# The halves of P exchanged between VectorE and GpSimd, and GpSimd's small work spread

## The chip, the core and the metric

One core of a Trainium2 chip runs the whole program. The metric is the device time of one execution in microseconds; the medians are over several runs. TensorE (PE in the profile) multiplies, VectorE (DVE), ScalarE (ACT) and GpSimd (POOL) work on elements, and SyncE (SP) issues nearly all DMAs. Each engine takes its instructions in the order in which the program has them, and waits for the others by semaphores that count up.

## What is computed

A cross attention with 16 heads over 64 batches of 128 queries (dimension 128) and 120 context rows, and behind it a feed-forward layer with 8 experts, in which each expert takes the 32 best tokens of a batch:

```python
q = _split_heads(queries @ Wq.T, N_HEAD, D_KEY)
k = _split_heads(keys @ Wk.T, N_HEAD, D_KEY)
v = _split_heads(values @ Wv.T, N_HEAD, D_VALUE)
scores = jnp.einsum('bhqd,bhkd->bhqk', q, k) * D_MODEL ** (-0.5) + attn_bias
weights = jax.nn.softmax(scores, axis=-1)
out = jnp.einsum('bhqk,bhkd->bhqd', weights, v)
...
gating, idx = jax.lax.top_k(affinity, k)
x_in = x[bidx, idx]
h = jax.nn.silu(jnp.einsum('bekd,eid->beki', x_in, w_gate)) * jnp.einsum('bekd,eid->beki', x_in, w_up)
...
x = x + _L0_xattn_ref(_layernorm(x, axis=-1), ctx_1024, ctx_1024, fside_1x1xSxS2_0, ...)
x = x + _L0_ffn_ref(_layernorm(x, axis=-1), ...)
```

## The kernel before

**Halves.** To multiply in float16 at nearly the precision of float32, a value is split into an upper half, its cast to float16, and a lower half, the value less the upper one. A product is then three matmuls. The names end in `_hi` and `_lo`. P (the exponentials of the scores, `probs`) and O (the attention's output, `o_sb`) are split as well, and both halves of both lie in one tensor `parts` for each of four groups, which a DMA transposes into `w_f` (`turned`).

**Batches, groups, steps.** The attention stage runs over slots t, one for each batch; in a slot four steps g = 0 to 3, one for each group of four heads. The scores and P of batch t - 1 are made in slot t. `behind(t, g, k)` is the group that lies k steps behind: O = PV runs 4 steps behind P (`PV_LAG`), its split 5, the projection 8. Slots up to 4 are written out, those from 5 to 62 are a loop that does two in a pass, and the last are written out again. Each engine has its own `step` or `slot`, and its order is the order of that code:

- **SyncE** (`turn`, L228; `load_x`, L207; `load_ffn`, L218). In slot t: turn(t, 0), load x and ctx of batch t + 2, turn(t, 1), load a piece of the experts' weights, turn(t, 2), turn(t, 3). `turn` of group g waits for the lower half of P of that group (`p_lo_ready`) and of the O that goes with it, and for what is still read from the place that it writes.
- **VectorE** (L454). Step 0 begins with bn_stats of x of batch t + 1 (L464), which waits for `loaded_xc`, both loads of that batch. Every step has four fused operations that make `neg` (scale, bias and row minimum, L472, with a read of the accumulator each); step 0 then has the aggregates mv (L488), step 1 xn (L494) and, for an earlier batch, xn2 (L536), and every step the reciprocal of P's row sums, v_lo (L514), o_sb (L522) and, last, the lower half of P of the group one step behind (L542).
- **GpSimd** (L298). In slot t, one after the other: the lower half of O (`lower_o`), eps added to the variance (vpe), rstd by a power, ctx_hi, the scaled piece of weights wsc (L326), the upper half of P of group 0 (`upper_parts`, L287), O again, ctx_lo, xn_hi, xn_lo, P of group 1, O, ffn_hi, xg_hi, P of group 2, O, ffn_lo, xg_lo, P of group 3. It waits for its own results by the counter `pool_chain`, whose values `chain` works out.
- **ScalarE** (L391). In each step v_hi and qk from PSUM, the upper half of O (L419), and four Exp for P (L443), which wait for `neg` and for the lower half of the group two steps back, in whose buffer they write. Steps 3 and 0 have copies for the transposes and the logits.
- **TensorE** (L579). In each step the scores (L590), V, the projection, PV and then Q and K.

Behind the attention stage (to about 743 us) come the routing and the experts' stage (from about 786 us to the end). There the subtract of 128x512 elements (L1133) runs on GpSimd.

Of the kernel before, what the change touches and what calls it, by code (L numbers as in the profile page):

```python
# [5 lines left out]
ALU = mybir.AluOpType  # L6
# [67 lines left out]
def attention(nc, v):  # L74
# [8 lines left out]
    with ExitStack() as ctx:  # L83
# [177 lines left out]
        @block.gpsimd  # L261
        def _(pool):
            pool.memset(ident[:, :], 0.0).then_inc(pool_chain, 1)
            pool.memset(half[:, :], -0.5).then_inc(const_ready, 1)
            pool.memset(vpe[:, :], 1.0).then_inc(const_ready, 1)
            pool.memset(mv[:, :, :], 1.0).then_inc(const_ready, 1)
            for i in range(2):
                pool.memset(v_hi[i][:, :, DH:OW], 1.0).then_inc(const_ready, 1)
            for i in range(GROUPS):
                pool.memset(parts[i][:, :, :], 0.0).then_inc(const_ready, 1)  # L270
            pool.wait_ge(pool_chain, 1)
            pool.affine_select(out=ident[:, :], in_=ident[:, :], compare_op=ALU.not_equal, fill=1.0,
                               base=0, pattern=[[-1, 128]], channel_multiplier=1).then_inc(const_ready, 1)
            pool.iota(iota[:, :], pattern=[[1, 128]], base=0, channel_multiplier=0,
                      allow_small_or_imprecise_dtypes=True).then_inc(const_ready, 1)
            pool.wait_ge(const_ready, 11)
            pool.tensor_copy(ident_h[:, :], ident[:, :]).then_inc(ident_h_ready, 1)

            def upper_parts(t, g):

                if live(t - 1):
                    n = 4 * (t - 1) + g
                    pool.wait_ge(probs_ready, n + 1)
                    if some(t - 1):
                        pool.wait_ge(moved[g], 16 * (t - 1))
                    alone(pool)
                    pool.tensor_copy(p_parts[g][:, 0, :, 0:K], probs[g % 2][:, :, :]).then_inc(p_hi_ready, 1)  # L287

            def lower_o(t, g):

                b5, g5 = behind(t, g, SPLIT_LAG)
                if live(b5):
                    n = 4 * b5 + g5
                    pool.wait_ge(o_hi_ready, n + 1)
                    pool.tensor_tensor(o_parts[g5][:, 1, :, :], o_sb[g5 % 2][:, :, :], o_parts[g5][:, 0, :, :],  # L295
                                       ALU.subtract).then_inc(o_lo_ready, 1)

            def slot(t, par):  # L298
                c = chain(t)
                at = slice(t * WCH, (t + 1) * WCH) if isinstance(t, int) else bass.ds(t * WCH, WCH)  # L300
                i = (par + 1) % 2
                lower_o(t, 0)

                pool.wait_ge(stats_ready, t + 2)
                alone(pool)
                pool.tensor_scalar(vpe[:, :], mv[:, :, 1], EPS, None, ALU.add).then_inc(pool_chain, 1)
                pool.wait_ge(pool_chain, c[0])
                if some(upto(t + 1)):
                    pool.wait_ge(xn_ready, upto(t + 1))
                if some(t - 4):  # L310
                    pool.wait_ge(xn2_ready, t - 4)
                pool.tensor_tensor(rstd[:, :], vpe[:, :], half[:, :], ALU.pow).then_inc(rstd_ready, 1)
                if live(t + 1):

                    pool.wait_ge(loaded_xc, (t + 2) * 32)
                    if some(4 * t):
                        pool.wait_ge(v_written, 4 * t)
                    alone(pool)
                    pool.tensor_copy(ctx_hi[i][:, :], ctx_f[i][:, :]).then_inc(pool_chain, 1)
                if live(t):  # L320

                    if some(t):
                        pool.wait_ge(ffnw_ready, t)
                    pool.wait_ge(loaded_ffn, (t + 1) * 16)
                    alone(pool)
                    pool.tensor_scalar(wsc[:, :], wst[par][:, :], WSCALE, None, ALU.mult).then_inc(pool_chain, 1)  # L326
                upper_parts(t, 0)
                lower_o(t, 1)
                if live(t + 1):

                    pool.wait_ge(pool_chain, c[1])
# [8 lines left out]
                    pool.wait_ge(pool_chain, c[3])  # L340
# [3 lines left out]
                if live(t):  # L344

                    pool.wait_ge(pool_chain, c[2])
                    alone(pool)
                    pool.tensor_copy(ffn_hi[:, at], wsc[:, :]).then_inc(pool_chain, 1)
                if live(t - 4):

                    pool.wait_ge(xn2_ready, t - 3)
                    alone(pool)
                    pool.tensor_copy(xg_hi[:, t - 4, :], xn2[:, :]).then_inc(pool_chain, 1)
                upper_parts(t, 2)
                lower_o(t, 3)
                if live(t):
                    pool.wait_ge(pool_chain, c[4])
                    pool.tensor_tensor(ffn_lo[:, at], wsc[:, :], ffn_hi[:, at], ALU.subtract).then_inc(ffnw_ready, 1)
                if live(t - 4):
                    pool.wait_ge(pool_chain, c[5])  # L360
                    pool.tensor_tensor(xg_lo[:, t - 4, :], xn2[:, :], xg_hi[:, t - 4, :],
                                       ALU.subtract).then_inc(xg_ready, 1)
                upper_parts(t, 3)

            def chain(t):

                def before(lag, each):
                    return each * (t - lag) if not isinstance(t, int) else each * min(max(t - lag, 0), B)  # L370
                c = 1 + (t + 1) + before(-1, 2) + before(0, 2) + before(4, 1)
                out = [c + 1]
                for batch in (t + 1, t, t + 1, t, t - 4):
                    out.append(out[-1] + (1 if live(batch) else 0))
                return out

            slots(pool, slot)

        @block.scalar
        def _(act):  # L380
# [10 lines left out]
            def step(t, par, g):  # L391
# [42 lines left out]
                if gw == GROUPS - 1 and live(tw - 4):  # L434
                    act.wait_ge(logits_written, tw - 3)
                    nc.scalar.copy(logits[:, tw - 4, :], gate_out).then_inc(logits_ready, 1)
                if live(t - 1):

                    act.wait_ge(neg_ready, n + 1)
# [11 lines left out]
        def _(dve):  # L451
            dve.wait_ge(const_ready, 11)

            def step(t, par, g):  # L454
# [10 lines left out]
                if live(t - 1):  # L465
# [5 lines left out]
                    for i in range(GH):  # L471
# [38 lines left out]
                if live(tw):  # L510
# [3 lines left out]
                    nc.vector.tensor_tensor(v_lo[pw][0:K, at, :],  # L514
                                            bk_b[gw % 2][0:K, 0:GH * DH].rearrange("p (a b) -> p a b", a=GH),
                                            v_hi[pw][0:K, at, 0:DH], ALU.subtract).then_inc(v_lo_ready, 1)
                if live(b4):

                    dve.wait_ge(rsum_ready, 4 * b4 + g4 + 1)
# [10 lines left out]
                if g == 1 and live(t - 4):  # L530
# [7 lines left out]
                b1, g1 = behind(t, g, 1)  # L538
                if live(b1):
# [746 lines left out]
```

## Time and profile before

| | us |
|---|---|
| Median of three runs | 1086.35 (1084.44 to 1086.76) |
| The profiled execution | 1088.91, of it the span 1086.8 |
| TensorE busy | 1003.1 (92% of the span) |
| VectorE busy | 900.8 (83%) |
| GpSimd busy | 881.3 (81%) |
| ScalarE busy | 811.6 (75%) |

Instructions overlap at their ends: the next one on an engine starts 0.04 to 0.1 us before the recorded end of the one ahead. What one costs in a row of instructions is therefore read from start to start. A wait is given with what ended it. S0 below is the start of bn_stats in step 0 of a slot.

### The profile page before, as it was taken

How to read it: one execution, taken by the hardware profiler on the slowest of the kernel's cores; microseconds unless marked ns; L12 is line 12 of the kernel's file. 1: busy time of each engine (PE TensorE's matmuls, PEld its weight loads, DVE VectorE, ACT ScalarE, POOL GpSimd, SP SyncE). 2: the span in 40 equal slices, each digit the busy share in tenths (PEclk: the TensorE clock that was granted, in tenths of full speed). 3: DMA queues.
4: the chain of work that ended last, by engine and by line, in shares of the span. 5: the costliest groups of instructions: out<-in, count | busy, mean ns of one | idle time of the engine just before them, and what ended most of it. 6: DMA issues, size and time to landing. Idle time of an engine off the chain costs nothing. (4 is left out here: it accounts for less than half of the span.)

```text
span 1086.8 us, 47397 instructions
## 1 busy us (share of the span) xinstructions
PE 1003.1 (92%) x13640; PEld 810.8 (75%) x13640; DVE 900.8 (83%) x3848; ACT 811.6 (75%) x2408; POOL 881.3 (81%) x1411
## 2 busy tenths in 40 slices
PE   4889999999999999999999999984799999999995
PEld 3777888888888888888888888873366666666664
DVE  4999999999999999999999999994756565665553
ACT  5887888888888888888888888871476667566562
POOL 7789999999999999999999999983077767677673
PEclk9999999999999999999999999995599999999998
DMA  3998887888888887888888888882001121111112
GB/s 101 161 152 157 162 167 154 169 160 163 162 159 163 165 164 154 166 160 162 161 160 162 164 167 158 170 153 49 1 21 29 30 67 30 39 55 32 50 49 68
DMA packets 440585, 130.91 MB, mean 120 GB/s; under 512 B 417504, under 2 KB 433888, under 8 KB 440544
## 3 DMA queue, kind: packets, MB, share of 16 engines
q1 hardware_dynamic: 439680, 128.24, 60.7%
q10 hardware_dynamic: 864, 2.16, 0.6%
q8 instruction: 21, 0.34, 0.1%
q14 instruction: 20, 0.16, 0.1%
HBM read 16.58 MB, written 4.19 MB: 19 GB/s over the span
## 5 line engine op out<-in xcount | busy, mean ns | idle before, releaser
L443 ACT ACTIVATE probs<-neg,negmax 128x120 f32<-128x120 f32 x1024 | 320.8, 386 | 109.0 <-DVE negmax L472 108.7
L472 DVE CUSTOM_DVE_ANT_0 neg<-bk_s,bias_sb 128x120 f32<-128x120 f32 x1024 | 225.9, 274 | 3.1 <-PE bk_s L590 2.3
L1133 POOL TENSOR_TENSOR hid<-hid_f,hid 128x512 f16<-128x512 f32 x128 | 167.7, 1313 | 74.9 <-ACT hid L1087 73.9
L542 DVE TENSOR_TENSOR parts<-probs,parts 128x480 f16<-128x480 f32 x256 | 210.8, 824 | 3.1 <-POOL parts L287 2.4
L590 PE MATMUL bk_s<-qk 64*128 64x120 f32 x2048 | 181.4, 295 | 12.5 <-DVE negmax L472 7.2
L295 POOL TENSOR_TENSOR parts<-o_sb,parts 128x256 f16<-128x256 f32 x256 | 172.1, 672 | 9.0 <-ACT parts L419 5.5
L590 PEld LDWEIGHTS bk_s<-qk 64*128 64x128 f32 x2048 | 136.2, 186 | 35.7 <-issue 18.1
L1187 DVE TENSOR_TENSOR hid_f<-bk_u,silu 128x512 f32<-128x512 f32 x128 | 88.3, 691 | 85.9 <-ACT silu L1080 35.0
L287 POOL CAST parts<-probs 128x480 f16<-128x480 f32 x256 | 150.5, 588 | 9.9 <-ACT probs L443 6.1
L411 ACT COPY qk<-bk_a 128x496 f32<-128x496 f32 x256 | 145.9, 570 | 2.3 <-PE bk_a L577 2.3
L633 PE MATMUL bk_o<-v_hi,w_f 120*128 120x65 f16 x1024 | 121.4, 196 | 0.6 <-DMA w_f<-parts 0.4
L635 PE MATMUL bk_o<-v_hi,w_f 120*128 120x65 f16 x1024 | 120.8, 193 | 0.0
L634 PE MATMUL bk_o<-v_lo,w_f 120*128 120x64 f16 x1024 | 120.3, 192 | 0.0
L575 PE MATMUL bk_a<-xT,w_hi 128*128 128x128 f16 x512 | 113.8, 222 | 5.2 <-ACT qk L411 2.6
L617 PE MATMUL bk_y<-wp_hi,w_f 128*128 128x128 f16 x512 | 101.5, 223 | 16.4 <-DMA w_f<-parts 14.6
L577 PE MATMUL bk_a<-xT,w_hi 128*128 128x128 f16 x512 | 112.3, 219 | 0.0
L576 PE MATMUL bk_a<-xT,w_lo 128*128 128x128 f16 x512 | 112.2, 219 | 0.0
L419 ACT CAST parts<-o_sb 128x256 f16<-128x256 f32 x256 | 105.2, 411 | 8.6 <-DVE o_sb L522 8.6
L1080 ACT ACTIVATE silu<-bk_g 128x512 f32<-128x512 f32 x128 | 78.1, 610 | 44.6 <-PE bk_g L970 43.3
L576 PE MATMUL bk_a<-ctx_hi,w_lo 128*128 128x120 f16 x512 | 111.0, 217 | 0.0
L577 PE MATMUL bk_a<-ctx_lo,w_hi 128*128 128x120 f16 x512 | 111.0, 217 | 0.0
L575 PE MATMUL bk_a<-ctx_hi,w_hi 128*128 128x120 f16 x512 | 110.9, 217 | 0.0
(166 smaller groups left out, 3591.3 us busy)
## 6 DMA issues: line engine op xcount, KB each, us to landing
y_all<-y SPq DMA_DIRECT2D x128, 64.0 KB, 2.0
wst<-ffn_w SPq DMA_DIRECT2D x64, 96.0 KB, 2.5
w_f<-parts SPq DMA_TRANSPOSE x260, 3.8
x_sb<-x SPq DMA_DIRECT2D x64, 64.0 KB, 2.3
out<-x_sb SPq DMA_DIRECT2D x16, 256.0 KB, 2.0
ctx_f<-ctx_t SPq DMA_DIRECT2D x64, 60.0 KB, 2.0
w_f<-wqkv_t ACTq DMA_DIRECT2D x3, 512.0 KB, 5.5
wp_sb<-wp_t ACTq DMA_DIRECT2D x1, 512.0 KB, 5.9
```

Source lines behind the costliest of these rows:

```text
L287: pool.tensor_copy(p_parts[g][:, 0, :, 0:K], probs[g % 2][:, :, :]).then_inc(p_hi_ready, 1)
L295: pool.tensor_tensor(o_parts[g5][:, 1, :, :], o_sb[g5 % 2][:, :, :], o_parts[g5][:, 0, :, :], ALU.subtract).then_inc(o_lo_ready, 1)
L411: nc.scalar.copy(qk[pw][:, gw, :], bk_a[:, 0:QK]).then_inc(qk_ready, 1)
L443: e = nc.scalar.activation(probs[g % 2][:, i, :], neg[g % 2][:, i, :], ACT.Exp, bias=negmax[g % 2][:, i:i + 1], scale=-1.0)
L472: r = nc.vector.tensor_tensor_reduce(out=neg[g % 2][:, i, :], in0=bk_s[i % 2][:, (i // 2) * K:(i // 2 + 1) * K], in1=bias_sb[:, :], scale= ...
L542: nc.vector.tensor_tensor(p_parts[g1][:, 1, :, 0:K], probs[g1 % 2][:, :, :], p_parts[g1][:, 0, :, 0:K], ALU.subtract).then_inc(p_lo_ready, 1)
L575: nc.tensor.matmul(out, lh, rh, start=True, stop=False)
L576: nc.tensor.matmul(out, ll, rh, start=False, stop=False)
L577: return nc.tensor.matmul(out, lh, rl, start=False, stop=True)
L590: m = nc.tensor.matmul(bk_s[h][:, j * K:(j + 1) * K], qk[p1][r, g, j * S:(j + 1) * S], qk[p1][r, g, GP * S + j * K:GP * S + (j + 1) * K], ...
L633: nc.tensor.matmul(bk_o[:, i * OW:(i + 1) * OW], ph, v_hi[p2][0:K, h, :], start=True, stop=False)
L1133: nc.gpsimd.tensor_tensor(hid[1][par][:, ic, :], hid_f[ic % 2][:, :], hid[0][par][:, ic, :], ALU.subtract).then_inc(hid_lo_ready, 1)
```

## The change

P's upper half is made by VectorE in place of GpSimd, and stands behind the `neg` operations of a step, for the group one step behind. P's lower half is made by GpSimd in place of VectorE (`lower_parts`), also one step behind, at the places where `upper_parts` stood. vpe moves from GpSimd to VectorE, between v_lo and o_sb of step 0. ffn_hi and xg_hi are made by ScalarE, ahead of the Exps of steps 1 and 2; ffn_hi is one activation with the scale, without the scaled copy wsc. ffn_lo is made by VectorE at the end of step 2, one operation that scales and subtracts. xg_lo stays on GpSimd. SyncE's and TensorE's code stay as they are.

```diff
@@ gpsimd
-            def upper_parts(t, g):
-
-                if live(t - 1):
-                    n = 4 * (t - 1) + g
-                    pool.wait_ge(probs_ready, n + 1)
-                    if some(t - 1):
-                        pool.wait_ge(moved[g], 16 * (t - 1))
+            def lower_parts(t, g):
+
+                b1, g1 = behind(t, g, 1)
+                if live(b1):
+                    pool.wait_ge(p_hi_ready, 4 * b1 + g1 + 1)
                     alone(pool)
-                    pool.tensor_copy(p_parts[g][:, 0, :, 0:K], probs[g % 2][:, :, :]).then_inc(p_hi_ready, 1)
+                    pool.tensor_tensor(p_parts[g1][:, 1, :, 0:K], probs[g1 % 2][:, :, :],
+                                       p_parts[g1][:, 0, :, 0:K], ALU.subtract).then_inc(p_lo_ready, 1)
...
-                pool.wait_ge(stats_ready, t + 2)
+                pool.wait_ge(vpe_ready, t + 2)
                 alone(pool)
-                pool.tensor_scalar(vpe[:, :], mv[:, :, 1], EPS, None, ALU.add).then_inc(pool_chain, 1)
-                pool.wait_ge(pool_chain, c[0])
...
-                    pool.tensor_scalar(wsc[:, :], wst[par][:, :], WSCALE, None, ALU.mult).then_inc(pool_chain, 1)
-                upper_parts(t, 0)
+                lower_parts(t, 0)
                 lower_o(t, 1)
...
-                upper_parts(t, 1)
+                lower_parts(t, 1)
                 lower_o(t, 2)
-                if live(t):
-
-                    pool.wait_ge(pool_chain, c[2])
+                lower_parts(t, 2)
+                lower_o(t, 3)
+                if live(t - 4):
+
+                    pool.wait_ge(xg_hi_ready, t - 3)
...
@@ scalar
+                if g == 1 and live(t):
...
+                    act.wait_ge(loaded_ffn, (t + 1) * 16)
+                    alone(act)
+                    nc.scalar.activation(ffn_hi[:, at], wst[par][:, :], ACT.Copy, scale=WSCALE).then_inc(ffn_hi_ready, 1)
+                if g == 2 and live(t - 4):
+
+                    act.wait_ge(xn2_ready, t - 3)
+                    alone(act)
+                    nc.scalar.copy(xg_hi[:, t - 4, :], xn2[:, :]).then_inc(xg_hi_ready, 1)
@@ vector
+                b1, g1 = behind(t, g, 1)
+                if live(b1):
+
+                    dve.wait_ge(probs_ready, 4 * b1 + g1 + 1)
+                    if some(b1):
+                        dve.wait_ge(moved[g1], 16 * b1)
+                    alone(dve)
+                    nc.vector.tensor_copy(p_parts[g1][:, 0, :, 0:K], probs[g1 % 2][:, :, :]).then_inc(p_hi_ready, 1)
                 if g == 0:
...
+                    nc.vector.tensor_scalar(vpe[:, :], mv[:, :, 1], EPS, None, ALU.add).then_inc(vpe_ready, 1)
...
-                    dve.wait_ge(p_hi_ready, 4 * b1 + g1 + 1)
-                    nc.vector.tensor_tensor(p_parts[g1][:, 1, :, 0:K], probs[g1 % 2][:, :, :],
-                                            p_parts[g1][:, 0, :, 0:K], ALU.subtract).then_inc(p_lo_ready, 1)
+                if g == 2 and live(t):
...
+                    dve.wait_ge(ffn_hi_ready, t + 1)
+                    alone(dve)
+                    nc.vector.scalar_tensor_tensor(out=ffn_lo[:, at], in0=wst[par][:, :], scalar=WSCALE, in1=ffn_hi[:, at],
+                                                   op0=ALU.mult, op1=ALU.subtract).then_inc(ffnw_ready, 1)
```

GpSimd in a slot, from eps to the P operation of step 1. The number behind `parts` is the group; in brackets the semaphores that an instruction waits for. Before:

```order
L306 TENSOR_SCALAR vpe<-mv 128x2 [waits stats_ready]
L312 TENSOR_TENSOR rstd<-vpe,half 128x2 [waits xn_ready,pool_chain]
L319 CAST ctx_hi1<-ctx_f1 128x120 [waits loaded_xc,v_written]
L326 TENSOR_SCALAR wsc<-wst0 128x192 [waits ffnw_ready,loaded_ffn]
L287 CAST parts0<-probs0 128x4x120 [waits probs_ready,moved0]
L295 TENSOR_TENSOR parts0<-o_sb0,parts0 128x256 [waits o_hi_ready]
L332 TENSOR_TENSOR ctx_lo1<-ctx_f1,ctx_hi1 128x120 [waits pool_chain]
L339 CAST xn_hi<-xn 128x128 [waits xn_ready,xT_written]
L341 TENSOR_TENSOR xn_lo<-xn,xn_hi 128x128 [waits pool_chain]
L287 CAST parts1<-probs1 128x4x120 [waits probs_ready,moved1]
```

The same stretch in the changed kernel:

```order
L310 TENSOR_TENSOR rstd<-vpe,half 128x2 [waits vpe_ready,xn_ready]
L317 CAST ctx_hi1<-ctx_f1 128x120 [waits loaded_xc,v_written]
L286 TENSOR_TENSOR parts3<-probs1,parts3 128x4x120 [waits p_hi_ready]
L295 TENSOR_TENSOR parts0<-o_sb0,parts0 128x256 [waits o_hi_ready]
L324 TENSOR_TENSOR ctx_lo1<-ctx_f1,ctx_hi1 128x120 [waits pool_chain]
L331 CAST xn_hi<-xn 128x128 [waits xn_ready,xT_written]
L334 TENSOR_TENSOR xn_lo<-xn,xn_hi 128x128 [waits pool_chain]
L286 TENSOR_TENSOR parts0<-probs0,parts0 128x4x120 [waits p_hi_ready]
```

The P operations are subtracts now and one group further back: the one behind ctx_hi makes group 3 of the batch before, and the one behind xn_lo group 0, for which `turn(t, 0)` waits. vpe and wsc are gone from the stretch.

VectorE in step 0, behind the `neg` operations. Before:

```order
L488 BN_AGGR mv<-stats 128x2 x2
L509 RECIPROCAL rsum<-bk_o 128x4
L514 TENSOR_TENSOR v_lo<-bk_b,v_hi 120x256
L522 TENSOR_TENSOR o_sb<-bk_o,rsum 128x256
L542 TENSOR_TENSOR parts<-probs,parts 128x4x120
```

The same place in the changed kernel:

```order
L472 CAST parts<-probs 128x4x120
L484 BN_AGGR mv<-stats 128x2 x2
L505 RECIPROCAL rsum<-bk_o 128x4
L510 TENSOR_TENSOR v_lo<-bk_b,v_hi 120x256
L519 TENSOR_SCALAR vpe<-mv 128x2
L525 TENSOR_TENSOR o_sb<-bk_o,rsum 128x256
```

The operation on P is a cast now and has moved from the end of the step to the front of it, ahead of the aggregates; vpe has come in ahead of o_sb.

## Rows read from the trace of the kernel before

**Rows 1.** Busy time of each engine in a stretch of the attention loop, times in us.

```profile
core 0: us, PE busy (x) PEld busy (x) DVE busy (x) ACT busy (x) POOL busy (x), PEclk, DMA share, GB/s
400.00:500.00 100.00, 97.06 (x1521) 85.36 (x1521) 97.16 (x494) 84.77 (x278) 92.50 (x171) 1.00 0.85 162
```

**Rows 2.** Waits of VectorE, 200 to 700: us in total, times, longest.

```profile
DVE stats L464 <- DMA ctx_f<-ctx_t: 9.0, 26, 0.6
DVE stats L464 <- issue: 0.5, 3, 0.2
DVE parts L542 <- POOL parts L287: 0.5, 1, 0.5
```

**Rows 3.** Timeline of VectorE: start, us, instruction, idle time before and releaser.

```profile
32.60 0.30 DVE L464 BATCH_NORM_STATS2 stats<-x_sb 128x6 f32<-128x128 f32 x1 [1.26 <-DMA ctx_f<-ctx_t]
...
401.08 0.29 DVE L464 BATCH_NORM_STATS2 stats<-x_sb 128x6 f32 x1 [0.34 <-DMA ctx_f<-ctx_t]
...
402.22 0.24 DVE L488 BATCH_NORM_AGGREGATE mv<-stats 128x2 f32<-128x6 f32 x2
...
402.78 0.41 DVE L522 TENSOR_TENSOR o_sb<-bk_o,rsum 128x256 f32<-128x256 f32 x1
...
406.06 0.89 DVE L542 TENSOR_TENSOR parts<-probs,parts 128x480 f16<-128x480 f32 x1
...
412.41 0.29 DVE L464 BATCH_NORM_STATS2 stats<-x_sb 128x6 f32 x1 [0.51 <-DMA ctx_f<-ctx_t]
...
700.94 0.29 DVE L464 BATCH_NORM_STATS2 stats<-x_sb 128x6 f32 x1 [0.59 <-DMA ctx_f<-ctx_t]
```

**Rows 4.** Timeline of SyncE's queue, and the landing of ctx's loads, 200 to 700.

```profile
402.14 6.68 SPq L247 DMA_TRANSPOSE w_f<-parts  x3
409.15 0.60 SPq L212 DMA_DIRECT2D x_sb<-x  x1
410.07 0.33 SPq L216 DMA_DIRECT2D ctx_f<-ctx_t  x1
...
DMA to landing us min/median/max: 1.8/2.0/2.3
```

**Rows 5.** Timeline of GpSimd in the same batch.

```profile
402.62 0.22 POOL L306 TENSOR_SCALAR vpe<-mv 128x2 f32<-128x2 f32 x1 [0.35 <-DVE mv L488]
403.01 0.72 POOL L312 TENSOR_TENSOR rstd<-vpe,half 128x2 f32<-128x2 f32 x1 [0.17 <-POOL vpe L306]
403.69 0.28 POOL L319 CAST ctx_hi<-ctx_f 128x120 f16<-128x120 f32 x1
404.06 0.71 POOL L326 TENSOR_SCALAR wsc<-wst 128x192 f32<-128x192 f32 x1
404.83 0.58 POOL L287 CAST parts<-probs 128x480 f16<-128x480 f32 x1
405.38 0.67 POOL L295 TENSOR_TENSOR parts<-o_sb,parts 128x256 f16<-128x256 f32 x1
406.01 0.41 POOL L332 TENSOR_TENSOR ctx_lo<-ctx_f,ctx_hi 128x120 f16<-128x120 f32 x1
406.38 0.71 POOL L339 CAST xn_hi<-xn 128x128 f16<-128x128 f32 x1
407.17 0.43 POOL L341 TENSOR_TENSOR xn_lo<-xn,xn_hi 128x128 f16<-128x128 f32 x1
407.54 0.58 POOL L287 CAST parts<-probs 128x480 f16<-128x480 f32 x1
...
409.42 0.29 POOL L353 CAST xg_hi<-xn 128x128 f32 x1
409.66 0.58 POOL L287 CAST parts<-probs 128x480 f16<-128x480 f32 x1
```

**Rows 6.** Durations by line, ns min/median/max: two subtracts of GpSimd, and L542.

```profile
L1133 POOL TENSOR_TENSOR hid<-hid_f,hid x128: 1153/1160/2142, 786.6 to 1068.3; 128x512 f16<-128x512 f32 x128
...
L295 POOL TENSOR_TENSOR parts<-o_sb,parts x181: 663/672/711, 199.5 to 698.7; 128x256 f16<-128x256 f32 x181
...
L542 DVE TENSOR_TENSOR parts<-probs,parts x181: 642/770/1130, 200.4 to 699.6; 128x480 f16<-128x480 f32 x181
```

**Rows 7.** Timelines of VectorE and GpSimd: xg_lo beside L542, twice.

```profile
411.14 0.76 DVE L542 TENSOR_TENSOR parts<-probs,parts 128x480 f16<-128x480 f32 x1
...
411.35 0.84 POOL L361 TENSOR_TENSOR xg_lo<-xn,xg_hi 128x128 f32 x1
...
721.44 0.43 POOL L361 TENSOR_TENSOR xg_lo<-xn,xg_hi 128x128 f16<-128x128 f32 x1
...
721.47 0.92 DVE L542 TENSOR_TENSOR parts<-probs,parts 128x480 f16<-128x480 f32 x1
```

**Rows 8.** Busy time and granted clock in three stretches, columns as in rows 1.

```profile
22.00:27.00 5.00, 3.75 (x47) 2.80 (x45) 4.09 (x20) 3.95 (x12) 3.95 (x7) 1.00 0.01 3
27.00:32.00 5.00, 4.04 (x52) 3.22 (x53) 3.97 (x21) 3.79 (x13) 2.91 (x7) 1.00 0.63 122
...
729.00:732.00 3.00, 1.08 (x20) 0.99 (x20) 1.78 (x11) 1.73 (x7) 2.19 (x4) 0.98 0.88 136
```

**Rows 9.** Timeline of TensorE: scores of two steps.

```profile
400.02 0.71 PE L590 MATMUL bk_s<-qk 64*128 64x120 f32 x8 [0.24 <-issue]
...
402.48 0.71 PE L590 MATMUL bk_s<-qk 64*128 64x120 f32 x8
```

More of the change, by code:

```diff
@@ L105, in attention @@
         wst = two("wst", [D, WCH], F32)
-        wsc = sb("wsc", [D, WCH], F32)
         stats = sb("stats", [S, 2, 6], F32)
@@ L149, in attention @@
         ctx_ready, ffnw_ready = sem("ctx_ready"), sem("ffnw_ready")
+        ffn_hi_ready, xg_hi_ready = sem("ffn_hi_ready"), sem("xg_hi_ready")
+        vpe_ready = sem("vpe_ready")
         pool_chain = sem("pool_chain")
@@ L299, in slot @@
                 c = chain(t)
-                at = slice(t * WCH, (t + 1) * WCH) if isinstance(t, int) else bass.ds(t * WCH, WCH)
                 i = (par + 1) % 2
                 lower_o(t, 0)
-                pool.wait_ge(stats_ready, t + 2)
+                pool.wait_ge(vpe_ready, t + 2)
                 alone(pool)
-                pool.tensor_scalar(vpe[:, :], mv[:, :, 1], EPS, None, ALU.add).then_inc(pool_chain, 1)
-                pool.wait_ge(pool_chain, c[0])
                 if some(upto(t + 1)):
@@ L311, in slot @@
                     pool.wait_ge(xn2_ready, t - 4)
+                alone(pool)
                 pool.tensor_tensor(rstd[:, :], vpe[:, :], half[:, :], ALU.pow).then_inc(rstd_ready, 1)
@@ L319, in slot @@
                     pool.tensor_copy(ctx_hi[i][:, :], ctx_f[i][:, :]).then_inc(pool_chain, 1)
-                if live(t):
[L322 to L325, printed above, removed]
-                    pool.tensor_scalar(wsc[:, :], wst[par][:, :], WSCALE, None, ALU.mult).then_inc(pool_chain, 1)
-                upper_parts(t, 0)
+                lower_parts(t, 0)
                 lower_o(t, 1)
                 if live(t + 1):
-                    pool.wait_ge(pool_chain, c[1])
+                    pool.wait_ge(pool_chain, c[0])
+                    alone(pool)
                     pool.tensor_tensor(ctx_lo[i][:, :], ctx_f[i][:, :], ctx_hi[i][:, :],
@@ L339, in slot @@
                     pool.tensor_copy(xn_hi[:, :], xn[:, :]).then_inc(pool_chain, 1)
-                    pool.wait_ge(pool_chain, c[3])
+                    pool.wait_ge(pool_chain, c[1])
+                    alone(pool)
                     pool.tensor_tensor(xn_lo[:, :], xn[:, :], xn_hi[:, :], ALU.subtract).then_inc(xn_parts_ready, 1)
-                upper_parts(t, 1)
+                lower_parts(t, 1)
                 lower_o(t, 2)
-                if live(t):
-                    pool.wait_ge(pool_chain, c[2])
+                lower_parts(t, 2)
+                lower_o(t, 3)
+                if live(t - 4):
+                    pool.wait_ge(xg_hi_ready, t - 3)
                     alone(pool)
[L348 to L360, printed above, removed]
                     pool.tensor_tensor(xg_lo[:, t - 4, :], xn2[:, :], xg_hi[:, t - 4, :],
                                        ALU.subtract).then_inc(xg_ready, 1)
-                upper_parts(t, 3)
+                lower_parts(t, 3)
             def chain(t):
[L369 to L375, printed above, removed]
+                hi = 2 * (t + 1) if not isinstance(t, int) else 2 * min(t + 1, B)
+                return [1 + hi + (k if live(t + 1) else 0) for k in (1, 2)]
             slots(pool, slot)
@@ L436, in step @@
                     nc.scalar.copy(logits[:, tw - 4, :], gate_out).then_inc(logits_ready, 1)
+                if g == 1 and live(t):
+                    at = slice(t * WCH, (t + 1) * WCH) if isinstance(t, int) else bass.ds(t * WCH, WCH)
+                    act.wait_ge(loaded_ffn, (t + 1) * 16)
[5 more added lines that the diff above has]
+                    nc.scalar.copy(xg_hi[:, t - 4, :], xn2[:, :]).then_inc(xg_hi_ready, 1)
                 if live(t - 1):
@@ L516, in step @@
                                             v_hi[pw][0:K, at, 0:DH], ALU.subtract).then_inc(v_lo_ready, 1)
+                if g == 0:
+                    dve.wait_ge(stats_ready, t + 2)
+                    if some(t + 1):
+                        dve.wait_ge(rstd_ready, t + 1)
+                    alone(dve)
+                    nc.vector.tensor_scalar(vpe[:, :], mv[:, :, 1], EPS, None, ALU.add).then_inc(vpe_ready, 1)
                 if live(b4):
@@ L537, in step @@
                                             ALU.subtract, ALU.mult).then_inc(xn2_ready, 1)
-                b1, g1 = behind(t, g, 1)
-                if live(b1):
-                    dve.wait_ge(p_hi_ready, 4 * b1 + g1 + 1)
-                    nc.vector.tensor_tensor(p_parts[g1][:, 1, :, 0:K], probs[g1 % 2][:, :, :],
-                                            p_parts[g1][:, 0, :, 0:K], ALU.subtract).then_inc(p_lo_ready, 1)
+                if g == 2 and live(t):
+                    at = slice(t * WCH, (t + 1) * WCH) if isinstance(t, int) else bass.ds(t * WCH, WCH)
+                    dve.wait_ge(ffn_hi_ready, t + 1)
+                    alone(dve)
+                    nc.vector.scalar_tensor_tensor(out=ffn_lo[:, at], in0=wst[par][:, :], scalar=WSCALE, in1=ffn_hi[:, at],
+                                                   op0=ALU.mult, op1=ALU.subtract).then_inc(ffnw_ready, 1)
                 if isinstance(t, int) and t == 1 and g == 0:
```

## The prediction

> **What bounds the kernel now.** I read the busy shares by stretch first, then the waits of VectorE in the loop over the batches, then the timelines of VectorE, SyncE and GpSimd over one batch. In the attention loop TensorE (97%), VectorE (97%) and GpSimd (92%) are all nearly full [rows 1], so shares don't name the bound. A batch is four steps (g = 0 to 3). The one thing that VectorE waits for there, 9.0 us in 26 of 45 batches, is the load of the next batch at bn_stats, L464, its first instruction of step 0 [rows 2]. I call its start S0.
>
> That wait closes a **loop of one period through four engines**. SyncE issues in order: the transpose of P's group 0 (`turn(t, 0)`) stands ahead of `load_x(t + 2)`, and that transpose waits for the lower half of group 0, L542, at the end of VectorE's step 1. In the batch that starts at 401.08: L542 of step 1 starts at 406.06 and takes 0.89, so ends at 406.95, S0 + 5.87 [rows 3]. Then come the transpose, the load of x at 409.15 and that of ctx at 410.07 [rows 4]; the next bn_stats starts at 412.41, after idling 0.51 on that load [rows 3]. So S0 to S0 is 5.87 + 5.46 = 11.33 us. Over the whole loop, (700.94 - 32.60) / 60 = 11.14 us for a batch [rows 3]. VectorE's own work is only a few tenths shorter: both limits lie together.
>
> **Part by part, against that loop.**
>
> *P's halves exchanged.* The lower half of group 0 is now made by GpSimd, in its part of step 1, behind everything that stands ahead of it in GpSimd's order: rstd, ctx_hi, the lower half of the group before, O's lower half, ctx_lo, xn_hi, xn_lo. Starts in the trace of before, each to the next start [rows 5]: rstd 403.01 to 403.69, 0.68; O's lower half 405.38 to 406.01, 0.63; ctx_lo to 406.38, 0.37. ctx_hi to the next is 0.37, but part may be waiting; xg_hi, the same kind of cast in front of a P operation, is followed after 0.24 (409.42 to 409.66), so 0.3. xn_hi takes 0.79 there, of which 0.43 is contention (below): 0.37. xn_lo 0.37. No row has a subtract of 480 elements on GpSimd. The same operation takes 1160 ns on 512 elements in the expert stage and 672 on 256 here [rows 6], so (1160 - 672) / 256 = 1.9 ns an element: 1160 - 32 x 1.9 = 1.10 us, about 1.05 from start to start. From rstd to the end of group 0's lower half: 0.68 + 0.30 + 1.05 + 0.63 + 0.37 + 0.37 + 0.37 + 1.10 = **4.87 us**. Before, from rstd to the end of L542 in step 1: 406.95 - 403.01 = 3.94. So +0.93.
>
> *rstd starts later too.* eps is added on VectorE after the cast of P, the aggregates, the reciprocal and v_lo. S0 to the end of v_lo's slot is 402.78 - 401.08 = 1.70 now [rows 3]. The cast comes ahead of it; no row has a 480-element cast on VectorE. Its upper bound is the two-input operation that it replaces, 642 ns uncontended [rows 6], about 0.57 from start to start; its lower bound a VectorE operation on 128 elements in SBUF, 0.28 to 0.29 [rows 3]. A one-input cast may run at more than one element a cycle, so I take 0.4, nearer the lower. With 0.31 for it: 2.01, plus 0.13 for two elements (estimated from the aggregates' 0.24 for two) and 0.16 until GpSimd moves (mv ends at 402.46, vpe starts at 402.62 [rows 3, 5]): rstd at S0 + 2.30, and 2.40 with 0.4. Before it was 403.01 - 401.08 = 1.93. So +0.47; the bounds give +0.37 and +0.63.
>
> *SyncE's part is unchanged*, 5.46 us from the lower half to the next bn_stats. Sum: +0.47 + 0.93 = +1.40 us a batch, uncontended.
>
> The Trainium skill ("SBUF — State Buffer", Who interferes with whom) says that copies and casts of VectorE can enter a mode with two ports and then hold the pair shared with GpSimd as an exclusive lock for the whole instruction. That the pair is exclusive, the trace shows for two inputs; for a one-input cast no row does. By the rule the cast would block and be blocked every time, 0.4 in place of the 0.2, which makes 1189 us; without it 0, 1165.
>
> *Off the loop.* wsc, ffn_hi, ffn_lo, xg_hi and vpe leave GpSimd's order, most behind the point where the loop has left it: GpSimd's sum hardly changes (four casts at 0.55, wsc 0.77, ffn_hi, xg_hi, ffn_lo and vpe go; four subtracts at 1.05 come), and it then idles until the next eps. wsc (0.77) alone was inside the loop's path, and its leaving is already in the 4.87. ScalarE gets a 192- and a 128-element operation, some 0.5 us, at 85% busy [rows 1]; at a period of 12.6 its share is still under 80%, and Exp is behind negmax anyway. The multiply-subtract for ffn_lo stands at the end of VectorE's step 2, past the loop's exit. VectorE loses four times 0.57 and its waits and gains four casts: its work falls by up to 1 us, which **buys nothing** while it waits at bn_stats. P's buffer is free only after the lower half, so Exp of group 2 waits for the subtract of group 0 until about S0 + 7.8; Exp 1.2, then the cast of group 2 at about S0 + 9, and the end of step 3 by 10.5: before the next S0 at 12.7, so hidden, by 2 us or less.
>
> **The sum.** +1.40 + 0.2 = +1.60 us on a batch that already waited for its load. In 19 of 45 batches VectorE did not wait, so the loop there was a little shorter than the period: I take off 0.1. 60 periods x 1.5 = +90 us. The routing and expert stages don't change. The profiled execution took 1088.9 us (span 1086.8); with +90 it is 1179. The runs' median is 1086.35, 2.6 lower: **1177 us**.
> Bounds: low, +0.37 + 0.93 and off it 0.3 for the batches without a wait, +1.0 x 60 = +60: 1146. High, +0.63 + 0.93 + 0.43 = +2.0 x 60 = +120: 1206.
>
> **Rivals.**
> *VectorE's relief decides (faster).* If the load were not what S0 waits for, or the lower half not late, the period would be TensorE's own work. TensorE's step from scores to scores took 2.46 us where it hardly waited (400.02 to 402.48) [rows 9]; four of them and the transposes, some 0.5, are 10.3: -0.8 x 60 = -48, some 1040 us. For it: only 26 of 45 batches wait. Against: GpSimd's order puts 4.87 us between rstd and the lower half, which no engine can shorten. It needs a period under 11.1, so 1.5 us off a chain of single instructions. 8 in 100.
> *The two engines serialize (slower than forecast).* If each cast waits for the GpSimd instruction in progress (up to 1.05) and then holds it up, VectorE's steps grow to about 12 us and the chain by another 0.4 to 0.8 with xn late for xn_hi: period 12.9 to 14, 1195 to 1255. For it: GpSimd and L542 already block each other. 12 in 100.
> *The change does little.* If SyncE's part shrinks because transposes and loads are further apart, half of the added time might be given back: 1100 to 1146. The median landing of ctx is 2.0 us, at least 1.8 [rows 4], so there is little to give. 6 in 100, and 2 more for within 0.2%.
> *TensorE's clock falls.* It idles more, some 15 to 20% of a batch. The granted clock stayed at 1.00 with TensorE busy 3.75 of 5 and 4.04 of 5 us in the first batches, and left it only where it was busy 1.08 of 3 [rows 8]. At the lower level, 1.2 GHz, the loop would take over 1500 us. 2 in 100.
>
> **How the numbers follow.** The forecast has 70 in 100, from 1146 to 1206. The range for 8 in 10 adds most of the serializing case: 1140 to 1225. A difference of 0.2% is about what a measurement here can tell. Faster: 0.08, the first rival. Within 0.2%: 0.02. Slower: 0.90.
>
> **What would show it.** bn_stats at the head of step 0 waits for the load of ctx in nearly all batches, 1.5 us or more each, and VectorE falls to about 85% busy. Group 0's lower half ends about S0 + 7.3 to 7.6, and SyncE's tail is still 5.2 to 5.5. The subtract takes 1.10 to 1.15 us; the cast 0.4, or about 0.64 if it runs at one element a cycle. ACT waits for the lower half in step 2. GpSimd idles before rstd. I am wrong if the batch comes out under 12 us, if bn_stats doesn't wait, or if the lower half ends before S0 + 6.8.

## The result: 1186 us, 9% slower

| | before | changed |
|---|---|---|
| Median, us | 1086.55 (4 runs) | 1186.26 (4 runs) |
| Ratio | | 1.0915, 95% interval 1.0897 to 1.0932 |
| Profiled execution, us | 1088.91 | 1185.22 |
| Its span | 1086.8 | 1183.4 |
| The S0 at either end of 60 periods, us | 32.60 and 700.94 | 32.79 and 795.7 |
| One period | 11.14 | 12.72 |

The period is (795.7 - 32.79) / 60 = 12.72 us, 1.58 more than before, and 60 of them are 94.8 of the span's 96.6 us. The other 1.8 lie between the last bn_stats and the expert stage; that stage, from its first subtract on GpSimd to the end of the span, takes 300.2 us before and 299.6 after. One execution of the kernel before (1377.85 us) and one of after_short_sub (1231.99), both among the experiments' runs, were slow ones at a lower granted clock, and the ratios leave them out.

### The profile page after: what moved, and what is told of

Same layout as the page of the kernel before. It is cut to its first block and busy times, and to the rows that moved or that the text cites. A ratio compares the mean times of both kernels' runs of the same rounds, so it can differ in the third digit from the quotient of the medians.

```text
span 1183.4 us, 47647 instructions
## 1 busy us (share of the span) xinstructions
PE 1023.7 (87%) x13640; PEld 818.3 (69%) x13640; DVE 966.6 (82%) x3981; ACT 851.3 (72%) x2536; POOL 837.9 (71%) x1086
## 5 line engine op out<-in xcount | busy, mean ns | idle before, releaser
L286 POOL TENSOR_TENSOR parts<-probs,parts 128x480 f16<-128x480 f32 x256 | 291.7, 1139 | 3.1 <-DVE parts L472 3.0
L295 POOL TENSOR_TENSOR parts<-o_sb,parts 128x256 f16<-128x256 f32 x256 | 182.4, 712 | 77.3 <-ACT parts L396 77.2
L472 DVE CAST parts<-probs 128x480 f16<-128x480 f32 x256 | 173.1, 676 | 0.0
L310 POOL TENSOR_TENSOR rstd<-vpe,half 128x2 f32<-128x2 f32 x69 | 48.5, 702 | 121.4 <-DVE vpe L519 121.4
```

The costliest lines, as they stand in the source:

```text
L286: pool.tensor_tensor(p_parts[g1][:, 1, :, 0:K], probs[g1 % 2][:, :, :], p_parts[g1][:, 0, :, 0:K], ALU.subtract).then_inc(p_lo_ready, 1)
L472: nc.vector.tensor_copy(p_parts[g1][:, 0, :, 0:K], probs[g1 % 2][:, :, :]).then_inc(p_hi_ready, 1)
```

## The profile after

The same stretch as in [rows 1], then the waits from 200 to 700 us, all engines, that answer to [rows 2]. Times in us; in the second fence total, times, longest.

```profile
400.00:500.00 100.00, 88.06 (x1339) 75.95 (x1338) 93.92 (x447) 79.35 (x260) 76.26 (x111) 1.00 0.73 141
```

```profile
POOL rstd L310 <- DVE vpe L519: 69.2, 40, 2.2
ACT probs L431 <- DVE negmax L460: 52.3, 40, 1.7
ACT probs L431 <- POOL parts L286: 47.4, 79, 0.9
...
DVE stats L452 <- DMA ctx_f<-ctx_t: 27.9, 39, 1.0
```

TensorE fell from 97 to 88%, GpSimd from 92 to 76. GpSimd now idles 1.7 us a batch before rstd. VectorE waits at bn_stats (L452 now) in every batch, 0.72 us on average, where before it did in 26 of 45 and for 0.35. But VectorE is still 94% busy, and that I had not expected: by the busy rows its work in a batch rose from 0.972 x 11.14 = 10.8 to 0.939 x 12.72 = 11.9 us.

The timeline of VectorE over the batch that starts at 401.67 (without most `neg` operations and o_sb), against [rows 3]:

```profile
401.67 0.30 DVE L452 BATCH_NORM_STATS2 stats<-x_sb 128x6 f32 x1 [0.81 <-DMA ctx_f<-ctx_t]
402.08 0.28 DVE L460 CUSTOM_DVE_ANT_0 neg<-bk_s,bias_sb 128x120 f32<-128x120 f32 x1
...
402.90 0.41 DVE L472 CAST parts<-probs 128x480 f16<-128x480 f32 x1
403.22 0.24 DVE L484 BATCH_NORM_AGGREGATE mv<-stats 128x2 f32<-128x6 f32 x2
...
403.75 0.16 DVE L519 TENSOR_SCALAR vpe<-mv 128x2 f32<-128x2 f32 x1
...
404.96 0.48 DVE L472 CAST parts<-probs 128x480 f16<-128x480 f32 x1
405.37 1.11 DVE L490 TENSOR_SCALAR xn<-x_sb,mv,rstd 128x128 f32 x1
...
408.21 1.32 DVE L472 CAST parts<-probs 128x480 f16<-128x480 f32 x1
...
410.19 1.15 DVE L546 SCALAR_TENSOR_TENSOR ffn_lo<-wst,ffn_hi 128x192 f32 x1
...
412.07 0.59 DVE L472 CAST parts<-probs 128x480 f16<-128x480 f32 x1
...
414.52 0.29 DVE L452 BATCH_NORM_STATS2 stats<-x_sb 128x6 f32 x1 [0.73 <-DMA ctx_f<-ctx_t]
```

GpSimd in the same batch, against [rows 5]:

```profile
404.26 0.69 POOL L310 TENSOR_TENSOR rstd<-vpe,half 128x2 f32<-128x2 f32 x1 [1.98 <-DVE vpe L519]
404.90 0.28 POOL L317 CAST ctx_hi<-ctx_f 128x120 f16<-128x120 f32 x1
405.14 1.26 POOL L286 TENSOR_TENSOR parts<-probs,parts 128x480 f16<-128x480 f32 x1
406.36 0.67 POOL L295 TENSOR_TENSOR parts<-o_sb,parts 128x256 f16<-128x256 f32 x1
406.99 0.42 POOL L324 TENSOR_TENSOR ctx_lo<-ctx_f,ctx_hi 128x120 f16<-128x120 f32 x1
407.35 0.29 POOL L331 CAST xn_hi<-xn 128x128 f16<-128x128 f32 x1
407.78 0.43 POOL L334 TENSOR_TENSOR xn_lo<-xn,xn_hi 128x128 f16<-128x128 f32 x1
408.17 1.10 POOL L286 TENSOR_TENSOR parts<-probs,parts 128x480 f16<-128x480 f32 x1
409.23 0.84 POOL L295 TENSOR_TENSOR parts<-o_sb,parts 128x256 f16<-128x256 f32 x1
```

And SyncE's queue, against [rows 4]:

```profile
402.72 8.46 SPq L248 DMA_TRANSPOSE w_f<-parts  x3
411.51 0.59 SPq L213 DMA_DIRECT2D x_sb<-x  x1
412.41 0.33 SPq L217 DMA_DIRECT2D ctx_f<-ctx_t  x1
```

**The loop**, read from these rows: S0 at 401.67; rstd at 404.26, S0 + 2.59; the lower half of group 0, the subtract at 408.17, ends at 409.27, S0 + 7.60; the loads are issued at 411.51 and 412.41; the next S0 is 414.52, 5.25 behind the subtract's end. In the batch of before the two parts were 5.87 and 5.46. Both batches are on the long side of theirs. On average over the batches from 200 to 700 us (45 before, 40 after) rstd starts at S0 + 1.82 before and 2.44 after, from there to the end of the lower half it is 3.99 and 5.02, and from there to the next S0 5.29 and 5.24.

**The contention** is in the same rows. xn (L490) starts at 405.37 and ends at 406.48, right behind the end (406.40) of the subtract that GpSimd began at 405.14; without a rival it takes 0.34. The cast of step 2 starts at 408.21, 0.04 behind GpSimd's subtract, and ends at 409.53, again just behind it, 1.32 in place of 0.41; ffn_lo takes 1.15 in place of the 0.34 that it takes in the run "moves_only" below. VectorE loses so 0.9 + 0.2 + 0.1 (casts of steps 2, 3 and 1), 0.8 (xn) and 0.8 (ffn_lo), about 2.8 us a batch. GpSimd loses about 0.2 in a collision: L295 at 409.23 takes 0.84 against its usual 0.67.

## The experiments

Theory A is that of the prediction: the loop from the lower half of group 0 by way of SyncE's transpose and loads to bn_stats sets the period, and the change is slower since it makes that half later. Theory B is that the two engines that hold each other up set it, and that the wait at bn_stats only fills what is left. All ratios are to the kernel before, run on the same chip in the same rounds (its medians were 1086.55, 1087.37, 1088.39 and 1086.92 us).

| run | median, us | ratio (95%) | period, us |
|---|---|---|---|
| changed kernel | 1186.26 | 1.0915 (1.0897 to 1.0932) | 12.72 |
| after_loads_first | 1146.46 | 1.0542 (1.0517 to 1.0568) | 12.10 |
| before_loads_first | 1074.27 | 0.9876 (0.9851 to 0.9901) | 10.95 |
| after_pad_step3 | 1185.38 | 1.0916 (1.0881 to 1.0951) | 12.71 |
| after_pad_step0 | 1206.73 | 1.1092 (1.1063 to 1.1121) | 13.07 |
| moves_only | 1085.22 | 0.9972 (0.9956 to 0.9988) | 11.13 |
| exchange_only | 1235.23 | 1.1367 (1.1327 to 1.1406) | 13.54 |
| after_short_sub | 1104.47 | 1.0156 (1.0113 to 1.0200) | 11.42 |
| after_short_sub_loads_first | 1088.38 | 1.0008 (0.9996 to 1.0019) | 11.18 |
| moves_only_loads_first | 1056.11 | 0.9707 (0.9675 to 0.9740) | 10.68 |
| moves_loads_ffn_lo_pool | 1059.82 | 0.9749 (0.9733 to 0.9765) | 10.75 |

The period is worked out in each run as above, from the fourth bn_stats of the loop's line and the last one in the program, 60 batches later.

### The loads ahead of the transpose

```diff
             def slot(t, par):
                 for g in range(GROUPS):
-                    turn(t, g)
                     if g == 0 and live(t + 2):
                         load_x(t + 2, par)
+                    turn(t, g)
```

> The changed kernel, with SyncE's loads of x and ctx of batch t + 2 issued ahead of the transpose turn(t, 0) instead of behind it. Theory A (the loop lower half of group 0, transpose, loads, bn_stats sets the period): the wait of 0.72 us a batch at bn_stats (27.9 us in 39 batches) goes, and VectorE, which is busy for the remaining 11.9 us, becomes the limit: about 0.7 x 60 = 40 us less, 1140 to 1155 us. Theory B (VectorE and GpSimd hold each other up at the shared path, and the wait at bn_stats only fills what is left over): the wait goes but returns elsewhere, 1180 us or more.

Measured 1146.46, 40 us less than the changed kernel, as theory A had it. The busy row of 400 to 500 us, and the three longest waits from 200 to 700:

```profile
400.00:500.00 100.00, 90.97 (x1414) 79.16 (x1410) 99.15 (x471) 83.31 (x274) 80.16 (x116) 1.00 0.77 149
```

```profile
ACT probs L431 <- POOL parts L286: 56.2, 82, 1.0
POOL rstd L310 <- DVE vpe L519: 48.9, 42, 1.2
POOL parts L295 <- ACT parts L396: 47.4, 83, 0.6
```

The wait at bn_stats is gone and VectorE is full, 99%. So the loop set the period, and directly below it lies a second limit: VectorE, whose work fills 12.1 us (that collisions with GpSimd stretch it is shown by the short subtract below).

> The kernel before with the same reorder of SyncE. Theory A: its loop is also closed by that wait, but VectorE is only 9.0 us of 45 batches (0.2 a batch) short of full, so 5 to 12 us less: 1074 to 1082 us. Theory B: no difference, 1084 to 1089.

Measured 1074.27, 1.2% faster, with VectorE 99.8% busy from 400 to 500 us and no wait at bn_stats. The kernel before was closed by the same loop, and its own VectorE limit is 10.95. So the loop is not all of the change's loss: with the loads first in both kernels the changed one is still 72 us slower (1146.46 against 1074.27), by VectorE's longer work.

### One operation more, on the loop and off it

A memset of 400 float32 a partition on VectorE, once a batch. In after_pad_step3 it stands at the end of step 3:

```diff
+                if g == 3:
+                    nc.vector.memset(spare[:, :], 0.0)
```

In after_pad_step0 it stands ahead of the aggregates of step 0:

```diff
                 if g == 0:
+                    nc.vector.memset(spare[:, :], 0.0)
                     if live(t + 1):
```

> The changed kernel with one more VectorE operation a batch at the end of step 3, a memset of 400 float32 a row (some 0.45 us, no input in SBUF), past the point where the loop has left VectorE. Theory A: it fits in the 0.72 us that VectorE waits at the next bn_stats, so 0 to 5 us more (1186 to 1192). Theory B (VectorE's length sets the period): 0.45 x 64 = +29 us.

> The same memset, but in step 0 ahead of the aggregates, on the way from bn_stats to vpe and rstd. Theory A: it lengthens the loop by its full 0.45 us: +25 to +29 us, about 1213. Theory B: the same +29. Together with the pad in step 3 it tells the loop from plain length.

Behind the loop's exit the pad costs nothing (1185.38 against 1186.26); on the loop it costs 20 us. In after_pad_step3 it is taken out of the wait at bn_stats, which falls from 27.9 us in 39 batches to 9.5 in 29 (200 to 700 us). It is a memset of 0.39 us, here in after_pad_step0:

```profile
401.61 0.40 DVE L473 CAST parts<-probs 128x480 f16<-128x480 f32 x1
402.05 0.39 DVE L475 MEMSET spare<- 128x400 f32 x1
402.36 0.18 DVE L486 BATCH_NORM_AGGREGATE mv<-stats 128x2 f32<-128x6 f32 x2
402.46 0.15 DVE L507 RECIPROCAL rsum<-bk_o 128x4 f32<-128x4 f32 x1
```

From the cast to the aggregates it is 0.75 here against 0.32 in the changed kernel, and from the aggregates to the reciprocal 0.10 against 0.16: 0.37 more, by 60 is 22. That the same operation costs 20 us at one place and none at the other is what theory B can't give. I had put its price at 25 to 29: I took 0.45 us for the memset, and it adds 0.37 to the row.

### The exchange alone, and the rest alone

moves_only is the changed kernel with the upper half cast by GpSimd again, and the lower half subtracted at the end of VectorE's steps:

```diff
+                if live(b1):
+                    dve.wait_ge(p_hi_ready, 4 * b1 + g1 + 1)
+                    nc.vector.tensor_tensor(p_parts[g1][:, 1, :, 0:K], probs[g1 % 2][:, :, :],
+                                            p_parts[g1][:, 0, :, 0:K], ALU.subtract).then_inc(p_lo_ready, 1)
```

exchange_only is the kernel before with the lower half subtracted by GpSimd, and the upper half cast behind VectorE's `neg`:

```diff
+                    nc.vector.tensor_copy(p_parts[g1][:, 0, :, 0:K], probs[g1 % 2][:, :, :]).then_inc(p_hi_ready, 1)
```

> The change without the exchange: P's upper half stays on GpSimd and the lower on VectorE at their places of before; vpe, ffn_hi, xg_hi and ffn_lo are moved as in the change. Theory A (the exchange lengthens the loop, the moves don't): P's lower half of group 0 is again VectorE's, at S0 + 5.9 or a little sooner since GpSimd collides less. VectorE gets vpe (0.07) and ffn_lo (0.3 to 1.1) and is then the limit: 11.0 to 11.4 us a batch, 1080 to 1105 us. Rival (the moves carry the loss, by the waits that they add among the engines): over 1130.

> Only the exchange of P's halves; vpe, wsc, ffn_hi, ffn_lo and xg_hi stay on GpSimd. Theory A: the loop is that of the changed kernel plus wsc (0.77) and less what eps saves: S0 to rstd about 2.35, then 4.87 + 0.77, then 5.3: 13.3 us a batch; GpSimd's own sum of about 11.6 with collisions stays under it. 1215 to 1240 us, slower than the changed kernel. Rival (the moves carry the loss): under 1130.

Both times are in the range that theory A gave: the moves without the exchange are within 0.3% of before (0.9972), and the exchange alone is slower than the whole change by 49 us. In moves_only I had the limit wrong: not VectorE (96% busy from 400 to 500 us) but still the loop set the period, with a wait at bn_stats in 35 batches of the 500 us. So the exchange carries the loss and more, and the moves pay back a part of it. Most of that part should be wsc, which in exchange_only stands on the loop and takes 0.97 us of it from start to start; wsc was not moved by itself. GpSimd there:

```profile
401.79 0.72 POOL L311 TENSOR_TENSOR rstd<-vpe,half 128x2 f32<-128x2 f32 x1 [0.17 <-POOL vpe L305]
402.46 0.28 POOL L318 CAST ctx_hi<-ctx_f 128x120 f16<-128x120 f32 x1
402.83 0.88 POOL L325 TENSOR_SCALAR wsc<-wst 128x192 f32<-128x192 f32 x1
403.80 1.09 POOL L285 TENSOR_TENSOR parts<-probs,parts 128x480 f16<-128x480 f32 x1
...
406.59 1.27 POOL L285 TENSOR_TENSOR parts<-probs,parts 128x480 f16<-128x480 f32 x1
```

From rstd to the end of the second subtract it is 407.86 - 401.79 = 6.07 us there, 5.01 in the changed kernel.

In moves_only ffn_lo stands at the end of step 2 as in the changed kernel, and GpSimd idles when it starts (its next operation, a cast, starts at 408.91):

```profile
408.12 0.64 DVE L538 TENSOR_TENSOR parts<-probs,parts 128x480 f16<-128x480 f32 x1
408.69 0.34 DVE L545 SCALAR_TENSOR_TENSOR ffn_lo<-wst,ffn_hi 128x192 f32 x1
```

### A short subtract

```diff
-                    pool.tensor_tensor(p_parts[g1][:, 1, :, 0:K], probs[g1 % 2][:, :, :],
-                                       p_parts[g1][:, 0, :, 0:K], ALU.subtract).then_inc(p_lo_ready, 1)
+                    pool.tensor_tensor(p_parts[g1][:, 1, 0:1, 0:K], probs[g1 % 2][:, 0:1, :],
+                                       p_parts[g1][:, 0, 0:1, 0:K], ALU.subtract).then_inc(p_lo_ready, 1)
```

> The changed kernel with GpSimd's subtract on one head of four (120 elements in place of 480); the lower halves of the other three heads stay zero, so part of the computation is left out. Theory A: two of these subtracts lie on the loop, 2 x (1.10 - 0.41) = 1.4 us less, and VectorE's casts and xn wait less for GpSimd; the loop would be 11.2 and VectorE, without most of its 2.7 us of collisions, about 9.5 to 10.5, so the loop still sets it: about 11.1 us a batch, 1090 to 1105. Theory B: the same direction; it is the size on VectorE's casts (1.32 in step 2 now) that this run measures.

Measured 1104.47, at the slow end of what I had expected, with a period of 11.42: 1.30 less, where the two subtracts on the loop account for 1.4. The wait at bn_stats is still there (38.0 us in 44 batches), so the loop sets it. And VectorE's operations shrank though nothing in them was changed; the first fence is of the changed kernel, the second of this one, busy us and mean ns of one, 200 to 700:

```profile
L472 DVE CAST parts<-probs 128x480 f16<-128x480 f32 x158 | 108.3, 685 | 0.0
...
L546 DVE SCALAR_TENSOR_TENSOR ffn_lo<-wst,ffn_hi 128x192 f32 x39 | 44.7, 1147 | 0.0
```

```profile
L472 DVE CAST parts<-probs 128x480 f16<-128x480 f32 x177 | 86.5, 489 | 0.0
...
L546 DVE SCALAR_TENSOR_TENSOR ffn_lo<-wst,ffn_hi 128x192 f32 x44 | 22.5, 512 | 0.0
```

> The changed kernel with the loads ahead of turn(t, 0) and GpSimd's subtract on one head of four (three heads' lower halves stay zero: part of the computation is left out). With the loop gone, what is left is VectorE's length. If GpSimd's long subtracts are what stretches VectorE (casts, xn and ffn_lo wait 2.7 us a batch in the changed kernel), VectorE needs about 9.5 to 10 us here, and TensorE's 10.3 to 10.5 takes over: 1040 to 1060 us, 85 to 105 less than the 1146 us with the full subtract. If its length had other grounds, the time stays near 1100.

This one I missed: 1088.38, not 1040 to 1060. It is 58 us under the run with the full subtract (1146.46), and VectorE's work in a batch fell from 0.992 x 12.10 = 12.0 to 0.931 x 11.18 = 10.4 us, so the long subtracts are 1.6 us of its length; I had expected it to fall to 9.5 to 10. And VectorE is 93% busy there, not full: it waits for something else. Among the waits (200 to 600 us) are these:

```profile
DVE neg L460 <- PE bk_s L594: 18.5, 45, 0.6
PEld bk_y L621 <- DMA w_f<-parts: 18.3, 18, 1.0
PE bk_y L621 <- DMA w_f<-parts: 14.0, 18, 0.8
```

TensorE waits up to 1 us for a transposed `parts` in every other batch, and VectorE waits for scores, up to 0.6. That the second wait follows from the first is my reading and not shown. Which part of that chain (the lower half still late, the loads ahead of the transpose, or O's halves) makes the transpose late was not tried.

### Two versions that beat the kernel before

> The moves without the exchange, with the loads ahead of turn(t, 0). Theory A: nothing but VectorE's own length is left, which with vpe and ffn_lo is about 11.1: 1075 to 1095 us, at most level with the kernel before with the same reorder. It tells whether the small moves pay once the loop is gone.

Measured 1056.11, 2.9% faster than before, and beyond what I had expected (1075 to 1095). L538, the subtract that stayed on VectorE, takes 665 ns there against 849 in before_loads_first: with vpe, wsc, ffn_hi, ffn_lo and xg_hi gone from GpSimd, the two engines meet less. That is 4 x 0.18 = 0.7 us a batch, more than vpe and ffn_lo cost VectorE. The moves pay 18 us once the loop is open, and 3 us (0.3%) while it is closed.

The last edit takes ffn_lo out of VectorE's step 2 and gives GpSimd wsc behind O of step 2 and the subtract for ffn_lo behind O of step 3:

```diff
+                    pool.tensor_scalar(wsc[:, :], wst[par][:, :], WSCALE, None, ALU.mult).then_inc(wsc_ready, 1)
...
+                    pool.tensor_tensor(ffn_lo[:, at], wsc[:, :], ffn_hi[:, at], ALU.subtract).then_inc(ffnw_ready, 1)
```

> A version to beat both kernels: the moves without the exchange, the loads first (1056 us), and ffn_lo given back to GpSimd by way of wsc, in the places where GpSimd now idles before P's casts (68 us of waits for Exp in 47 batches). VectorE is full there (99.6%), ffn_lo costs it 0.27 to 0.3 us a batch: 16 to 18 us less, 1038 to 1042, if GpSimd's 1.3 us more don't collide with L538 (then 1050 to 1060).

Measured 1059.82, no gain and perhaps 4 us lost (the intervals of the two ratios overlap). The subtract of P on VectorE without and with the work on GpSimd (200 to 700, then 200 to 600):

```profile
L538 DVE TENSOR_TENSOR parts<-probs,parts 128x480 f16<-128x480 f32 x189 | 125.7, 665 | 0.0
```

```profile
L552 DVE TENSOR_TENSOR parts<-probs,parts 128x480 f16<-128x480 f32 x151 | 114.3, 757 | 0.0
```

VectorE saved some 0.27 us a batch (the operation for ffn_lo) and paid 4 x 0.09 = 0.37 for it.

## Why the prediction was right, point by point

- **The bound.** The loop of one period, with its four engines, is what set the time before and after: the loads moved ahead of the transpose took 40 us from the changed kernel and 13 from the one before, and the pad cost 20 us on the loop and none off it. The forecast of 1177 was 9 us (0.8%) short of 1186.
- **The subtract**, scaled from rows of other sizes [rows 6] to 1.10 us, measured 1088 to 1097 ns from the fastest to the median. rstd to the end of group 0's lower half: 4.87 and 0.2 of contention forecast, 409.27 - 404.26 = 5.01 measured, 0.17 of it the subtract at 405.14, which ran beside a cast. With 0.4 for contention in place of 0.2 my sum came to 1189 us, nearer to 1186 than 1177 is; but the rows have 0.17, so that nearness is luck.
- **rstd's start**: S0 + 2.40 forecast, 2.59 measured in this batch, from 2.28 to 2.59 over the batches of 200 to 700. The cast is cheaper than I took (0.32 from start to start, the lower end). But bn_stats to `neg` was 0.41 instead of 0.32, and from the end of vpe on VectorE (403.91) to rstd it was 0.35 us, not the 0.16 that I had taken from mv to vpe. rstd has three waits and two nops in front of it now; which of them costs was not tried. My lower bound for the cast was 0.28 to 0.29, but I worked its end of the range with 0.31; with 0.28 it would be +0.34 and not +0.37.
- **The sum**: 1.60 less 0.1 a period forecast, 1.58 measured. By the averages over the batches rstd came 0.62 later (0.47 forecast), the stretch from rstd to the lower half grew by 1.03 (1.13 with the contention), and SyncE's part shrank by 0.05 (0 forecast): the misses of +0.15, -0.10 and -0.05 cancel, which is luck. The 0.1 that I took off for the batches without a wait had nothing to stand for it, and made the forecast some 5 us short; 1.8 us between the last bn_stats and the expert stage and the offset between the profiled execution and the median (the median 2.6 below it forecast, 1.0 above it here) make up the rest.
- **What I mis-sized: VectorE's relief.** I had its work fall by up to 1 us and its share to 85%, with a wait of 1.5 us and more at bn_stats. The share was 94%, the wait 0.72, and the work rose by 1.1 us. What failed is the term for contention: I looked for it on GpSimd (0.2, about right) and on the cast of step 1, and not on VectorE's other operations. VectorE lost 2.8 us a batch: an operation that starts just behind a 1.1 us subtract waits for nearly all of it, as the cast of step 2 and xn do in the rows above. The rival "the two engines serialize" had the mechanism and VectorE's size (about 12 us), and missed the place: the waits of xn, of the later casts and of ffn_lo hold up nothing on the loop (xn ends at 406.48, and xn_hi starts at 407.35, behind ctx_lo) and were paid out of the wait at bn_stats. With the loads first they decide: 12.10 us a period against 10.95. The margin was 0.72 us a batch. That these waits would fit into it I had not worked out, so that they left the forecast alone is luck too.
- **Which operations share the path.** I had weighed at 0.2 whether a cast with one input would use the shared path. By the Trainium skill ("SBUF — State Buffer", Who interferes with whom) copies, casts and tensor_scalar can take it, and whoever starts second waits for the whole instruction. The trace agrees for a cast and for tensor_scalar: 1.32 and 1.11 us, each ended within 0.3 us behind GpSimd's subtract. The cast of step 1 (404.96), whose result the subtract at 408.17 needs, began 0.18 ahead of GpSimd's subtract and took 0.48; there it was the subtract that waited. The cast of step 0 found GpSimd idle.
- **Waits that I named**: ScalarE waits for the lower half, but in steps 1 and 2 (79 times in 40 batches), not in step 2 alone. GpSimd idles before rstd, as said. TensorE's granted clock stayed at 1.00 (2.4 GHz) from 400 to 500 us with TensorE 88% busy.

## What to carry to other kernels

A load that stands in an in-order queue behind a transfer is as late as that transfer's last producer, and the loop through it can set the period of a kernel whose engines all look full. Before work is exchanged between two engines, look at what the moved result releases and at what stands in front of it on its new engine; here a memset was free behind the loop's exit and cost 20 us on the loop, and one line moved in the queue's order gave 13 us before the change and 40 after it. But opening the loop only uncovers the next limit: 72 of the 100 us that the change cost stayed, as longer work of VectorE (1146.46 against 1074.27 with the loads first). And an idle GpSimd is not free room while VectorE is the bound: in the one run that tried it, what GpSimd was given came back as longer operations on VectorE.

## What was not expected of the hardware

- A VectorE operation with **one** tensor input from SBUF (a cast of 128x480, xn of 128x128) waits for a GpSimd subtract that began ahead of it: 1.32 in place of 0.41 us, 1.11 in place of 0.34.
- It waits in the same way for a GpSimd operation with one input. In the kernel before, xn that began 0.31 to 0.44 us behind wsc took 0.48 to 0.35 and ended 0.07 to 0.09 behind it, as xn ends 0.08 behind the subtract above. The row at 404.49 looks free, but ended 0.09 behind wsc's 404.77 [rows 5]:

```profile
404.49 0.37 DVE L494 TENSOR_SCALAR xn<-x_sb,mv,rstd 128x128 f32 x1
```

- Which of the two waits is not always told by the recorded starts. xn that began only 0.05 to 0.28 us behind wsc took 0.34 to 0.39 and ended 0.2 to 0.3 ahead of it, in the kernel before and in exchange_only, and in most of these cases it was wsc that took longer, up to 0.89 in place of 0.71. In exchange_only, beside the wsc at 402.83 shown above:

```profile
403.07 0.37 DVE L501 TENSOR_SCALAR xn<-x_sb,mv,rstd 128x128 f32 x1
```

  Behind the subtract xn waited at such distances too (0.22 to 0.27 in the changed kernel). Why the two operations differ here was not tried.
- A cast of 480 float32 to float16 on VectorE takes 0.40 us at the least, 0.32 from start to start, where a two-input subtract of the same size takes 0.64 and 0.57 in the kernel before.
